# Softmax attention's scores as seven Strassen block products for a pair of row tiles

## The reference

```python
x = x + attn_a(layernorm(x))          # stage A
x = x + ffn(layernorm(x))             # F1
x = x + attn_b(layernorm(x))          # B, touched by the change
x = x + ffn(layernorm(x))             # F2

def attn_b(x, W_q, W_k, W_v, W_o):    # 2 batches of 1024 rows, one head of 512
    Q, K, V = x @ W_q, x @ W_k, x @ W_v
    p = softmax(Q @ K.T / sqrt(512))  # 1024 x 1024 for each batch
    return (p @ V) @ W_o
def ffn(x, ...):                      # hidden width 1408
    return down(silu(gate(x)) * up(x))
```

## Time and profile before

| quantity | value |
|---|---|
| median of 3 runs | 984.0 us (983.82 to 984.02) |
| the profiled execution | 983.62 us, its span 981.9 us |
| PE busy | 959.8 us (98%) |
| DVE, ACT, POOL busy | 584.9, 406.1, 432.2 us |
| stage B: from, to, length | 487.9, 760.0, 272.1 us |

### The profile page before, as it was taken

One profiled execution on the slowest core, in us unless ns is written; L12 is line 12 of the kernel. 1 busy time (PEld: TensorE's weight loads), 2 busy tenths in 40 slices (PEclk: granted clock), 3 DMA queues, 4 the chain that ended last, 5 costly groups with the idle time before them and its releaser, 6 DMA issues.

```text
span 981.9 us, 12989 instructions
## 1 busy us (share of the span) xinstructions
PE 959.8 (98%) x4798; PEld 545.1 (56%) x4818; DVE 584.9 (60%) x1096; ACT 406.1 (41%) x790; POOL 432.2 (44%) x444
## 2 busy tenths in 40 slices
PE   7999999999999999999999999999999999999998
PEld 4888888888734444444444445544455444444443
DVE  7565666859767676776343443524455676766643
...
PEclk9999999999999999999999999999999999999999
...
DMA packets 12302, 26.05 MB, mean 27 GB/s; under 512 B 1744, under 2 KB 1744, under 8 KB 12240
## 3 DMA queue, kind: packets, MB, share of 16 engines
...
## 4 chain that ended last, share of the span: by engine, by line
PE 81%; DVE 8%; POOL 4%; issue 3%; ACT 2%; DMA 1%; SPq 0%; POOLq 0%; DVEq 0%; ACTq 0%
PE psum L1804 52%; PE psum L2029 13%; PE psum L2031 12%; PE psum L2157 1%; PE psum L1826 1%; POOL yt L810 1%; PE psum L1837 1%; DVE xn L1227 1%; POOL hid L769 1%; DMA wqk_raw<-wk 1%; DVE yt L1612 1%; POOL hid L773 1%; DVE xq L1250 1%; DVE xres L1395 1%; DVE state L1382 1%
## 5 line engine op out<-in xcount | busy, mean ns | idle before, releaser
L773 POOL TENSOR_TENSOR hid<-hid,hid_hi 128x512 f32<-128x512 f32 x88 | 102.7, 1167 | 97.6 <-DVE hid_hi L1547 97.6
L2029 PE MATMUL psum<-xf,w_gu 128*128 128x512 f16 x352 | 133.8, 380 | 1.9 <-DVE mids L1626 1.1
L2029 PE MATMUL psum<-xf,w_s 128*128 128x512 f16 x264 | 100.0, 379 | 1.4 <-ACT acc L1013 0.6
L2031 PE MATMUL psum<-xf,w_gu 128*128 128x512 f16 x264 | 100.1, 379 | 0.0
L624 POOL TENSOR_TENSOR xrstd<-xvar,minus_half 128x1 f32<-128x1 f32 x32 | 17.6, 566 | 122.9 <-DVE xvar L1221 122.9
L769 POOL TENSOR_TENSOR hid<-up,gate 128x512 f32<-128x512 f32 x44 | 56.0, 1273 | 29.3 <-ACT gate L1029 29.3
L1034 ACT ACTIVATE hid_lo<-hid 128x512 f16<-128x512 f32 x88 | 54.9, 624 | 33.5 <-POOL hid L773 33.5
L2031 PE MATMUL psum<-xq,w_s 128*128 128x512 f16 x176 | 66.7, 379 | 0.0
L2029 PEld LDWEIGHTS psum<-xf,w_gu 128*128 128x128 f16 x352 | 34.3, 98 | 56.4 <-ACT acc L1019 15.5
L1029 ACT ACTIVATE gate<-gate,sg_xs 128x512 f32<-128x512 f32 x44 | 31.7, 721 | 70.6 <-DVE gate L1530 70.5
L1547 DVE TENSOR_SCALAR hid_hi<-hid 128x512 f16<-128x512 f32 x88 | 37.6, 427 | 32.1 <-POOL hid L769 30.6
...
## 6 DMA issues: line engine op xcount, KB each, us to landing
...
```

The source lines that it names most:

```text
L773: nc.gpsimd.tensor_tensor(hid[:, :], hid[:, :], hid_part(hid_hi, j, half), ALU.subtract).then_inc(rest_done, 1)
L2029: nc.tensor.matmul(bank(use[0]), w, x_operand(piece, k, False), start=start and k == 0, stop=False, skip_group_check=not start)
L2031: last = nc.tensor.matmul(bank(use[0]), w, x_operand(piece, k, True), start=False, stop=k == 1, skip_group_check=not start)
```

## The change

The scores of two neighbouring tiles (a pair p, tiles 2p and 2p + 1) are now built together. The inner dimension is cut in halves and the 1024 columns in halves, and of the eight products of a 2 x 2 block product seven pieces remain (Strassen's scheme in Winograd's form). A piece is 128x512, two slices of the inner dimension, so 6 matmuls (`score(piece, p)`). Pieces 1, 6, 7 and 4 are summed in bank 4 one on top of the other, and after each of them ACT copies the running sum into one quarter of the pair's scores, `probs0` or `probs1` in SBUF (`part_sum`, 4 for each pair). Pieces 2, 5 and 3 go to bank 5, and DVE adds each to a quarter in SBUF (`part_add`, 3 for each pair). `row_max` and `softmax` therefore read and write SBUF. A product needs sums of both operands:

- The left ones, sums of query blocks: a query block of the first half is copied by ACT as float32 (`a_copy`, with bank drained), and when its partner of the second half is there ACT takes the high parts `a2_hi` and `a1_hi` (`a_highs`), DVE makes the sums s1, s2, s4 and the low part of a2 (`query_parts`, four instructions, the last of which drains the partner's bank), POOL makes s3, the low part of a1 and the low parts of all four sums, ACT their high parts (`s_high`). Two such steps make a half (four query blocks in the order 0, 2, 1, 3, in banks 0, 1, 0, 1).
- The right ones, T1 to T4 of the rows: stage B's rows are prepared as row pairs with `turn_x`, `x_copy`, `x_highs`, `x_second`, `x_34_high`, `x_34_low` and POOL's four steps, as those of the feed-forward blocks are. Six sets of rows (F0, F1, B0, B1, F2, F3) replace four. Set B0 is made in the tail of F1 batch 1, B1 inside batch 0 of stage B, F2 inside batch 1. The first half's queries of batch 1 are made at the end of batch 0. POOL makes three of the weight sums `w_s` again in batch 1 (their place in SBUF is used by rows in between).

The turned probabilities move to other buffers, since the memory is short: `pT(b, i)` names them. `turn_use` gives banks 4 and 5 to the last turning of batch 1. PE's order is now by pairs: turn an even tile, two pieces of the next pair, attend, turn the odd tile, three pieces, half an attend, two pieces, the other half. Where a row pair is turned and where `out_add` stands against the next `pT_low` changes with it. Matmuls and transposes on PE: 4018 where there were 4066.

The diff, cut to its core:

```diff
+NEXT_SET = (F1, B0, F3)
...
+    def score_use(piece, p):
+        return {1: (4, 4 * p), 6: (4, 4 * p + 1), 7: (4, 4 * p + 2), 4: (4, 4 * p + 3),
+                2: (5, 3 * p), 5: (5, 3 * p + 1), 3: (5, 3 * p + 2)}[piece]
+    def turn_use(b, i):
+        return (4, 16) if (b, i) == (1, BT - 1) else (2, i)
...
+                    nc.gpsimd.tensor_tensor(sf[:, 4 * P:6 * P].rearrange("p (q n) -> p q n", q=2),
+                                            rows_of(af[:, :], 0), rows_of(af[:, :], 1),
+                                            ALU.subtract).then_inc(s3_done, 1)
+                    pool.wait_ge(a1_hi_done, n + 1)
...
+                    nc.gpsimd.tensor_tensor(a1[1], rows_of(af[:, :], 0), a1[0], ALU.subtract).then_inc(a1_lo_done, 1)
...
+            x_rstd(F2, *range(8))
+            pool.wait_ge(x_34_lo, 4 * B1 + 4)
+            for dst, src, less in ((3, 7, 1), (4, 2, 0), (5, 3, 1)):
+                nc.gpsimd.tensor_tensor(cols(w_s, dst, HID), cols(w_gu, src, HID), cols(w_s, less, HID),
+                                        ALU.subtract).then_inc(ws_ready, 1)
+            query_parts(1, 1)
+            pairs_of(F2)
...
+                def part_sum(piece, p):
+                    use = score_use(piece, p)
+                    u.full(use)
+                    row, half = {1: (0, 0), 6: (0, 1), 7: (1, 1), 4: (1, 0)}[piece]
+                    nc.scalar.activation(cols(probs[row], half), bank(4), ACT.Copy).then_inc(drained[4], 1)
                 def softmax(i):
-                    u.full((4, i))
+                    r = slice(i % 4, i % 4 + 1)
                     act.wait_ge(nmax_done, b * 8 + (i + 1))
-                    nc.scalar.activation(probs[:, :], bank(4, 2), ACT.Exp, scale=s_scale[:, 0:1],
-                                         bias=nmax[:, i % 2:i % 2 + 1],
-                                         accum_out=rowsum[:, i % 2:i % 2 + 1]).then_inc(drained[4], 1)
+                    nc.scalar.activation(probs[i % 2][:, :], probs[i % 2][:, :], ACT.Exp, scale=s_scale[:, 0:1],
+                                         bias=nmax[:, r], accum_out=rowsum[:, r]).then_inc(probs_done, 1)
...
+                    if p < 3:
+                        part_sum(4, p + 1)
+                    if p in (1, 2):
+                        x_34_high(q, 2 * p - 2)
+                    if p < 3:
+                        softmax(2 * p + 2)
+                    if p == 1 or (p == 2 and b == 0):
+                        x_copy(q, 2 * p - 1)
+                        x_highs(q, 2 * p - 1)
...
+                nc.vector.scalar_tensor_tensor(out=part(0), in0=rows_of(q, 1), scalar=QDOWN, in1=rows_of(af[:, :], 1),
+                                               op0=ALU.mult, op1=ALU.add).then_inc(s1_done, 1)
...
+                nc.vector.tensor_tensor(part(1), part(0), rows_of(af[:, :], 0), ALU.subtract).then_inc(s2_done, 1)
...
+                nc.vector.scalar_tensor_tensor(out=part(3), in0=rows_of(q, 0), scalar=QDOWN, in1=part(1),
+                                               op0=ALU.mult, op1=ALU.subtract).then_inc(s4_done, 1)
+                nc.vector.scalar_tensor_tensor(out=cols(a2_lo, c), in0=q, scalar=QDOWN, in1=cols(a2_hi, c),
+                                               op0=ALU.mult, op1=ALU.subtract).then_inc(drained[job % 2], 1)
...
+                    x = cols(probs[row], half)
+                    nc.vector.tensor_tensor(x, bank(5), x, ALU.add).then_inc(drained[5], 1)
...
-                    nc.vector.reduce_max(smax[:, r], bank(4, 2), AX.X).then_inc(smax_done, 1)
+                    nc.vector.reduce_max(smax[:, r], probs[i % 2][:, :], AX.X).then_inc(smax_done, 1)
...
+                    if p < 3:
+                        part_add(3, p + 1)
+                        row_max(2 * p + 2)
+                        row_max(2 * p + 3)
+                    if p in (1, 2):
+                        x_34_low(q, 2 * p - 2)
+                    if p == 1 or (p == 2 and b == 0):
+                        x_second(q, 2 * p - 1)
+                    if p == 1:
+                        x_normalise(q, 2)
...
+                    out_add(2 * p + 1)
...
+                for p in range(4):
+                    turn_probs(2 * p)
+                    if p == 1:
+                        for n in range(4):
+                            query(b, 1, n)
+                    elif p < 3:
+                        score(1, p + 1)
+                        score(2, p + 1)
+                    elif b == 0:
+                        query(1, 0, 0)
+                        query(1, 0, 1)
+                    else:
+                        turn_both(3)
+                        turn_probs(7)
+                    attend(2 * p)
+                    if (b, p) != (1, 3):
+                        turn_probs(2 * p + 1)
+                    if p == 1:
+                        score(1, 2)
+                        score(2, 2)
+                    if p < 3:
+                        for piece in (6, 5, 7):
+                            score(piece, p + 1)
+                        if p > 0:
+                            turn_both(2 * p - 2)
+                        attend(2 * p + 1, 0, 4)
+                        score(3, p + 1)
+                        score(4, p + 1)
+                        if p == 1 or (p == 2 and b == 0):
+                            turn_both(2 * p - 1)
+                        attend(2 * p + 1, 4, 8)
+                    else:
+                        if b == 0:
+                            query(1, 0, 2)
+                            query(1, 0, 3)
+                        attend(7)
```

894 lines of the change are left out of this document (492 added, 402 removed).

## The result

| | before | changed |
|---|---|---|
| median | 983.92 us (983.82 to 984.02, 4 runs) | 990.04 us (989.31 to 991.15, 4 runs) |
| profiled execution, its span | 983.62, 981.9 | 990.13, 988.4 |
| ratio | | 1.0063, 95% interval 1.0051 to 1.0075 |

The change makes the kernel slower by 6 us where 1 us was forecast, and the time lies above the range of 981.0 to 988.5.

The account below looks back on a forecast made before the run. PE was taken to set the pace; 983.62 - 10.35 + 0.8 + 2.95 + 3.65 + 1.55 + 2.2 + 0.2 = 984.6 us profiled, 985.0 at the median, range 981.0 to 988.5.

Parts of the forecast that it names:

- The gain, 10.35: Softmax attention's scores on PE: 48 fewer matmuls at 0.216 us each, 10.35 us saved, all on the path.
- (a): Tail of F1 batch 1: now makes row pairs, so PE waits 1.0 us for xn instead of 0.2; +0.8 us.
- (b): Queries in banks 0, 1, 0, 1: PE waits for DVE's query parts, s2 held by POOL; 4 x 0.74 = +2.95 us.
- (c): Pair 1 to pair 2 of scores, both batches: tile 4's low part late behind DVE's list; waits 1.7 and 1.9, +3.65 us.
- (d): Last pair of batch 1: PE waits for tile 7's exponential, +1.55 us, then its low part behind out_add(6), +2.2 us.
- (e): Softmax of an even tile, pairs 0, 1 and 3: chain of 3.7 to 3.8 just fits 3.88 us cover; +0.2 us.
- the walk: The forecast's pass through places where PE waits for the end of another engine's list, pricing each wait.
- The clock: Rival, chance 0.03: granted clock drops in the new gaps; with 5 us of work at half clock, 990 us.
- POOL holds row_max: Rival, chance 0.10: row_max, now reading SBUF, is held by POOL steps in attention; 4.5 us more, 989.5 us.
- The softmax chain overruns: Rival, chance 0.13: even tiles' softmax late by 0.5 us at six places, from SBUF steps or busy DVE; 987.8 us.
- No holds: Rival, chance 0.22: POOL and DVE miss each other, so query waits cost 1.0 and tile 4's waits 2.2; 981.6 us.
- all hidden: Rival, chance 0.07: attention's query, tile 4 and last-pair waits find cover, only F1's tail wait is left; 974.5 us.

Follow-up runs that it names:

- The last kernel: Changed kernel with all five reorderings of engine lists, plus a quarter of tile 5's attend moved behind tile 6's turning in batch 1: 978.56 us, ratio 0.9946.
- step b: Changed kernel with POOL's low part of a1 held until DVE has made s4, at all query steps: 989.30 us, ratio 1.0051.

## Why the prediction was wrong

**The gain, 10.35: right.** Attention's PE time fell by that and by the transposes that moved out (1.75). The last kernel bears the sum out: 984.0 - 10.35 + 0.8 (a) + 3.5 of stands (0.98, four of the queries that add to 1.7, 0.44 and 0.38) + 0.4 of small ones = 978.4, measured 978.56.

**(a) +0.8: right.** PE waits 1.0 for xn in F1's second tail, by the stands 0.8 more than before.

**(b) +2.95: right in kind and place; the size by luck.** 0.73, 0.82, 0.73 and 0.73 are 3.0. Without the hold of the low part they are 1.7, where I had 1.0: the chain is 0.1 to 0.25 longer at each place than by the rows it was priced from. So the hold is worth 0.3 a place and not the 0.49 of the forecast, and the two errors cancel. That the trace agrees with the Trainium skill (SBUF — State Buffer, "SBUF: two separate sides") shows in the pair of listings under step b: the same two-input SBUF step takes 0.42 or 0.74. The held step ends 0.28 us behind POOL's, less than the 0.42 that it takes alone.

**(c) +3.65: right.** 1.80 and 1.58 are 3.4 (the forecast's own terms add to 3.55; 3.65 is rounded up on the way). The gap between the batches (0.2) is as forecast, and it is ACT's: its high part ahead of x_second has 512 columns in batch 0 (0.59 us) and 256 in batch 1 (0.37), while DVE needs 3.86 us in both from x_second to the start of the low part. The two normalisations took 1.44 us in batch 0 and 1.70 in batch 1, where 1.71 was taken for both; the wider last step of x_second in batch 0 (0.68 against 0.41) makes up for it.

**(d) +1.55 and +2.2: right in size** (1.63 and 2.22), incomplete in the first cause: tile 6's own splits were as late as the exponential, so the order of the two was not the remedy.

**(e) +0.2: right in size, at another place.** No turning of an even tile waited for its exponential. Two stands of 0.2 stand ahead of the first attend of each batch, where two pieces (2.59) cover both splits of tile 0. Row_max over SBUF took 1.22 and the exponential 1.23, as priced.

**The failed step is a place that isn't in the walk.** The wait of batch 1's first query was put at nothing. Of these queries the walk says only that they "have an attend between them", which is about their banks, and of POOL it prices only the three weight sums, "with over 15 us to spare"; neither looks at the queries' input. They moved from inside batch 1 to the end of batch 0, where the last row pair of that batch has only just been turned, and their first wait, on POOL's low part, is the longest of all: 2.80 us. The rows for it were there: at the row pair of the earlier trace rows POOL's first sum starts 1.42 us after ACT's second step (726.33 to 727.75) and takes 0.73, and a second sum and the low part stand behind it in its list; all that follows the exponential of tile 6 on ACT, while PE has half an attend and one turning, 3.5 us. 985.0 + 2.8 = 987.8, where the two executions at full clock took 988.6, 0.8 more.

**The clock was a rival at 0.03 and came true.** Its price was put at 5 us of work at half clock; in the runs it is 1.3 to 1.7 us for a fall, in six of eight executions of the changed kernel. I rested on the full clock of before through its own gaps; in attention and the tails those gaps are under 1 us, and one of 1.61 us, added to it, still left the clock alone. Behind the one of 2.99 it fell in four of five. 987.8 + 0.8 + 1.5 = 990.1, measured 990.04, where the 0.8 is what full-clock executions have over the sum, without a cause.

**POOL holds row_max: void.** All sixteen maxima over SBUF took 1.208 to 1.221 us, and four of them ran beside a POOL pass. One is in DVE's timeline in the changed kernel:

```profile
609.95 1.22 DVE L1896 TENSOR_REDUCE smax<-probs 128x1 f32<-128x1024 f32 x1
```

POOL's at the same time:

```profile
609.87 1.16 POOL L721 TENSOR_TENSOR xs_lo<-x_mid,xs_hi 128x512 f16<-128x512 f32 x1
```

So the trace agrees with the Trainium skill (VectorE: DVE Perf Modes, "The perf-mode tier table"), which gives a reduction the 1x mode alone. **The softmax chain overruns: void** (no such wait). **No holds, all hidden: void.** The answer "slower" came from none of the two rivals on that side.

**What stays open.** Some 0.5 to 0.8 us of the difference at full clock. The profiled execution of the changed kernel was 0.6 us behind the one of before already ahead of F1's second batch, where nothing is changed. It differs from execution to execution: a turning in the tail of F1's first batch (at 353.58 in it, 352.94 before) lies at 352.82 to 353.49 in the seven other traces of reordered or repeated changed kernels whose clock held at the start. And the clock fell in two traces at 15 us, in kernels whose code there is that of before, whose 46 runs beside them all had 0.999 or 1.0. There PE had waited 1.91 and 2.14 us for the low part of the first rows; in the eleven other traces, in which the clock held there, that wait was 0.75 to 1.30. Why it was longer in those two isn't shown.
